# Attention mask of a tile written into two PSUM banks by VectorE and ScalarE in place of two matmuls

## The chip, the cores and the metric

The program runs on one core of a Trainium2 chip. The metric is the device time of one execution in microseconds (us). The engines that matter here are TensorE (PE in the profile, its weight loads PEld), VectorE (DVE), ScalarE (ACT), GpSimd (POOL) and the DMA queue that SyncE issues to (SPq). They run side by side, each through its own list of instructions in program order, and wait for each other by semaphores.

## What is computed

The reference is a chain of four residual blocks on x of 4 x 512 tokens x 128 channels. Two of the four are the same 6-layer stack of windowed attention and a gated MLP, and they take most of the time; only their attention matters for this change:

```
x = x + gla(layernorm(x)); x = x + stack(layernorm(x))
x = x + mamba(layernorm(x)); x = x + stack(layernorm(x))

# one attention layer of the stack: 16 heads of 64, windows of w = 32 tokens,
# each window's queries look at its own and the previous window's keys
mask = (it < jb) | (it > jb + w) | (jb == -1)
sim = jnp.einsum('bhwie,bhwje->bhwij', bq, bk2) * QK_SCALE
sim = jnp.where(mask, -jnp.finfo(sim.dtype).max, sim)
attn = jax.nn.softmax(sim, -1)
out = jnp.einsum('bhwij,bhwje->bhwie', attn, bv2)
```

The mask depends on the position inside the window alone, and on whether a window is the first of its sequence (it has no previous window). In the kernel a masked place gets -1e30 added.

## The kernel before

**The stack as units.** A stack handles 6 layers x 4 sequences = 24 iterations (`it`), each of 4 tiles of 128 tokens. One tile of one iteration is a unit `u`, so a stack has 96 units and the program 192. `pe_body`, `act_body`, `dve_body` and `pool_body` write out, for each engine, the work of one iteration. In the body of unit u stand pieces of several units, software-pipelined: the projections of q, k, v (`pe_proj`, chunks c = 0 to 5 of 512 columns, lines 273 to 275) of units u+2 and u+3, the transposes of q and k (`pe_qk_t`, line 286) and the scores (`pe_scores`, line 320) of unit u+1, and the transposed probabilities (`pe_probs_t`, line 301), the product with v (`pe_pv`, line 335) and the output projection (`pe_wo`, line 372) of units u and u-1. The MLP of the iteration before is spread over the same bodies (lines 378 to 403). The order is fixed by these functions; nothing is scheduled at run time.

**The banks.** PSUM has eight banks of 128 x 512 f32. `proj_ps` (banks 0, 1) takes the projection chunks in turn, `tr_ps` (2, 3) the transposes, `s_ps[0]` and `s_ps[1]` (4, 5) the scores of the even and of the odd heads of a unit, `o_ps` (6, 7) the rest.

**The scores of a unit.** `pe_scores(.., half 0)` waits until q and k of the unit stand transposed in SBUF (`qkT_ev`), and until the two score banks are free: `s_ps[0]` once VectorE has subtracted the row maximum (`sub_done`, line 775), `s_ps[1]` once ScalarE has taken the exponentials of the odd heads (`exp1_done`, line 571). Line 313 then starts each bank with a matmul of 512 columns: a one-hot matrix (it picks the row of the mask for each query) times the mask's rows, in bf16, one on the upper and one on the lower 64 rows of the array. 64 small matmuls of line 320 add the scores of four heads of each parity onto it, and 64 more (half 1) those of the others. VectorE then reduces both banks to the row maximum (line 770), ScalarE takes the exponentials (571, 578), VectorE sums and inverts (782, 786), GpSimd normalizes (934).

**v and the DMA queue.** `act_v` (line 535) copies the two v chunks of unit u+2 out of `proj_ps`; after the second, SyncE issues 16 DMAs (line 1035) that lay v out by window, and the first v copy of the next unit waits for them to land (`vp0` to `vp3`).

**The order around the change.** On ScalarE, in the body of u: copies of q transposed (554, `q_t`), the square of chunk 2 (527), the copies of k transposed (554, `k_t`), the square of chunk 3. On VectorE: rotation of chunk 1 (736, 738), the residual add (796, 797), rotation of chunks 2 and 3, the reciprocal norm (759 to 764), then the row maximum (770).

Of the kernel before, what the change touches and what calls it, by code (L numbers as in the profile page):

```python
# [20 lines left out]
BF16 = mybir.dt.bfloat16  # L21
I32 = mybir.dt.int32
ALU = mybir.AluOpType
ACT = mybir.ActivationFunctionType
# [54 lines left out]
def build(nc, a):  # L79

    ctx = ExitStack()
    with ctx:  # L82
# [13 lines left out]
        onehot = sb("onehot", [P, 2, P], BF16)  # L96
        maskrow = sb("maskrow", [P, CH], BF16)
        eps_t = sb("eps_t", [P, 1])
        rsq_3kk = sb("rsq_3kk", [P, 2 * HEADS])
        CONSTS = ((ident, "ident"), (center, "center"), (mean, "mean"), (onehot, "onehot"), (maskrow, "maskrow"))  # L100
# [103 lines left out]
        def mamba_buffers():  # L204
# [44 lines left out]
            "qkT_ev", "s_mm", "max_done", "sub_done", "den_sum", "exp1_done", "exp0_done", "den_done", "pT_mm", "pT_ev",  # L249
# [55 lines left out]

        def pe_scores(it, u, half):

            t = u % TILES
            if half == 0:
                nc.tensor.wait_ge(S["qkT_ev"], cnt(it, 4, u, 4))  # L310
                for g in range(2):
                    wait(nc.tensor, S["exp1_done" if g else "sub_done"], cnt(it, 1, u))
                    nc.tensor.matmul(s_ps[g], onehot[64 * g:64 * g + 64, 1 if t == 0 else 0, :],
                                     maskrow[64 * g:64 * g + 64, :], start=True, stop=False,
                                     skip_group_check=True)
# [264 lines left out]

        def act_center(e, src=o_ps[0]):
# [53 lines left out]
        def act_body(layer, j, mlp, ahead, more, norm=False):  # L635

            it = layer * B + j
            for u in range(TILES):
# [5 lines left out]
                if proj:  # L644
                    act_square(it, u + 2, 2)
                if nxt:
                    act_qk_t(it, u + 1, (2, 3))
# [130 lines left out]

        def dve_den(it, u):
# [54 lines left out]
        def dve_body(layer, j, mlp, ahead, norm=False):  # L834

            it = layer * B + j
            for u in range(TILES):
# [12 lines left out]
                elif prev:  # L850
                    dve_wo(it, u - 1)
                if proj:
                    dve_rotate(layer, j, u + 2, (2, 3))
# [953 lines left out]
def constants():  # L1807
# [22 lines left out]
    maskrow = np.zeros((64, HC, 2 * WIN), np.float32)  # L1830
    maskrow[:WIN] = np.concatenate([prev, own], 1)[:, None, :]
    maskrow[WIN, :, :WIN] = MASKED
    onehot = np.zeros((64, 2, P), np.float32)
    onehot[:WIN] = np.tile(np.eye(WIN), (1, WPT))[:, None, :]
    onehot[WIN, 1, :WIN] = 1.0
# [4 lines left out]
    for i in range(1, P // BC):  # L1840
        for n in range(BC):
            bc[i * BC + n, n, :] = 1.0
    return {"gla_pick": pick, "mb_bc_pick": bc.astype(bf), "rot": np.ascontiguousarray(rot), "maskrow": np.tile(maskrow.reshape(64, CH), (2, 1)).astype(bf),
            "onehot": np.tile(onehot, (2, 1, 1)).astype(bf), "ident": np.eye(P, dtype=np.float32),
# [62 lines left out]
```

## Time and profile before

| what | value |
|---|---|
| median of 3 runs | 3710.29 us (3702.14 to 3711.01) |
| the profiled execution, its own time | 3706.15 us |
| its span in the trace | 3704.4 us |
| mean granted TensorE clock, share of full | 0.978 |
| busy share of the span | PE 93%, PEld 67%, DVE 79%, ACT 74%, POOL 74% |

A busy share is an average over stages. The two stacks lie at about 140 to 1730 us and 2070 to 3680 us of the span; the other two blocks lie before and between them. A PE row's length is that of one instruction through the array, and instructions overlap in it, so what an instruction costs PE is read from the start of one row to the start of the next.

### The profile page before, as it was taken

What the parts mean: (1) busy time and instruction counts of PE and PEld (TensorE: products, weight loads), DVE (VectorE), ACT (ScalarE), POOL (GpSimd) and SP (SyncE); (2) the same over time, 40 slices, a digit from 0 to 9 for tenths busy, and PEclk for the clock granted to TensorE, in tenths of its full rate; (3) what the DMA queues carried; (4) which work ended last, traced back from release to release, by engine and by line L of the source; (5) the groups of instructions that cost most, each with busy time, mean ns of one, the idle gap of its engine ahead of it and who ended that gap; (6) DMA issues with size and microseconds to landing.
All of it is one profiled execution on the core that took longest, in us unless ns stands there. A gap on an engine that the chain in (4) does not pass through costs nothing. (4 is left out here: it accounts for less than half of the span.)

```text
span 3704.4 us, 152641 instructions
## 1 busy us (share of the span) xinstructions
PE 3447.7 (93%) x62652; PEld 2472.5 (67%) x62652; DVE 2934.0 (79%) x4676; ACT 2727.1 (74%) x7154; POOL 2739.4 (74%) x3122
## 2 busy tenths in 40 slices
PE   8799999999999999998887799999999999999996
PEld 3477777777777777775332577777777777777774
DVE  7688888888888888784999788888888878778773
ACT  2477878788787877776665578787787887777774
POOL 3587878787787878773666688787787878778772
PEclk9899999999999999999999899999999999999998
DMA  1232333333332333322000233332332333323321
GB/s 42 57 76 68 83 78 77 77 81 74 82 81 68 88 76 76 79 73 67 0 1 0 51 75 77 75 82 72 82 78 68 86 74 77 81 69 76 80 73 36
DMA packets 182839, 251.51 MB, mean 68 GB/s; under 512 B 53380, under 2 KB 74504, under 8 KB 182024
## 3 DMA queue, kind: packets, MB, share of 16 engines
q1 hardware_dynamic: 182152, 241.78, 26.2%
q8 instruction: 500, 8.19, 1.0%
q14 instruction: 187, 1.53, 0.1%
HBM read 39.20 MB, written 1.05 MB: 11 GB/s over the span
## 5 line engine op out<-in xcount | busy, mean ns | idle before, releaser
L959 POOL TENSOR_TENSOR qk_rows<-rot_products 128x512 f32<-128x512 f32 x768 | 983.0, 1281 | 223.2 <-DVE rot_products L736 222.6
L736 DVE TENSOR_TENSOR rot_products<-psum,rot_scaled 128x1024 f32<-128x1024 f32 x768 | 936.3, 1219 | 148.5 <-ACT squares L527 125.8
L969 POOL TENSOR_TENSOR qk_rows<-qk_rows,rnorm 128x512 f32<-128x512 f32 x768 | 803.7, 1078 | 15.0
L273 PE MATMUL psum<-wqkv_hi,xs_hi 128*128 128x512 f32 x1152 | 560.4, 486 | 89.3 <-DVE rot_products L736 37.3
L527 ACT ACTIVATE squares<-psum 128x512 f32<-128x512 f32 x768 | 488.4, 636 | 42.0 <-PE psum L275 36.6
L738 DVE TENSOR_REDUCE sumsq<-squares 128x8 f32<-128x512 f32 x768 | 518.2, 675 | 0.0
L535 ACT ACTIVATE v_rows<-psum 128x512 f32<-128x512 f32 x384 | 228.0, 595 | 367.8 <-DMA v_pairs<-v_rows 188.8
L934 POOL TENSOR_TENSOR probs<-probs,rden 128x512 f32<-128x512 f32 x384 | 393.3, 1045 | 92.4 <-DVE rden L786 91.5
L571 ACT ACTIVATE probs<-psum,minus_row_max 128x64 f32<-128x64 f32 x1536 | 457.1, 335 | 5.0 <-DVE minus_row_max L770 4.9
L275 PE MATMUL psum<-wqkv_hi,xs_lo 128*128 128x512 f32 x1152 | 459.6, 399 | 0.2 <-issue 0.2
L274 PE MATMUL psum<-wqkv_lo,xs_hi 128*128 128x512 f32 x1152 | 459.6, 399 | 0.0
L335 PEld LDWEIGHTS psum<-probs_t,v_pairs 64*64 64x64 f32 x24576 | 389.8, 136 | 103.0 <-issue 102.4
L335 PE MATMUL psum<-probs_t,v_pairs 64*64 64x32 f32 x24576 | 416.8, 221 | 27.7 <-issue 25.7
L372 PEld LDWEIGHTS psum<-o_t,wo 128*128 128x128 f32 x3072 | 362.9, 192 | 83.4 <-ACT o_t L543 60.3
L372 PE MATMUL psum<-o_t,wo 128*128 128x128 f32 x3072 | 388.2, 280 | 22.7 <-ACT o_t L543 16.4
L286 PE MATMUL psum<-ident,qk_rows 128*128 128x128 f32 x3072 | 402.9, 274 | 0.7 <-ACT q_t L554 0.5
L286 PEld LDWEIGHTS psum<-ident,qk_rows 128*128 128x128 f32 x3072 | 357.3, 142 | 29.9 <-issue 3.6
L320 PEld LDWEIGHTS psum<-k_t,q_t 64*32 64x32 f32 x24576 | 269.9, 105 | 151.4 <-issue 150.8
L571 ACT ACTIVATION_READ_ACCUMULATOR probs<-psum,minus_row_max 128x1 f32 x1536 | 353.8, 230 | 0.0
L273 PEld LDWEIGHTS psum<-wqkv_hi,xs_hi 128*128 128x128 f32 x1152 | 218.6, 190 | 187.6 <-issue 108.5
L320 PE MATMUL psum<-k_t,q_t 64*32 64x64 f32 x24576 | 332.4, 224 | 0.0
L770 DVE TENSOR_REDUCE minus_row_max<-psum 128x16 f32<-128x1024 f32 x192 | 234.3, 1220 | 115.9 <-PE psum L320 115.8
(188 smaller groups left out, 5995.3 us busy)
## 6 DMA issues: line engine op xcount, KB each, us to landing
v_pairs<-v_rows SPq DMA_DIRECT2D x3072, 64.0 KB, 2.0
wqkv_staged<-in_Wqkv SPq DMA_DIRECT2D x52, 384.0 KB, 3.6
wo<-in_Wo SPq DMA_DIRECT2D x12, 512.0 KB, 4.6
w<-in_W SPq DMA_DIRECT2D x12, 341.0 KB, 3.5
qk_scale<-in_qk_scale SPq DMA_DIRECT2D x12, 128.0 KB, 3.4
w<-in_W SPq DMA_DIRECT2D x12, 128.0 KB
mb_bc_pick<-in_mb_bc_pick SPq DMA_DIRECT2D x1, 1024.0 KB
out_x<-qk_rows SPq DMA_DIRECT2D x1, 1024.0 KB, 5.1
```

The lines of the kernel that those rows point to most:

```text
L273: nc.tensor.matmul(proj_ps[c % 2], xh, wh, start=True, stop=False)
L274: nc.tensor.matmul(proj_ps[c % 2], xh, wl, start=False, stop=False)
L286: last = nc.tensor.transpose(tr_ps[g % 2][:, i * P:(i + 1) * P], m["qk"][:, u % 2, (4 * g + i) * P:(4 * g + i + 1) * P], ident[:, :])
L320: last = nc.tensor.matmul(s_ps[par][WIN * w:WIN * w + WIN, 64 * hp:64 * hp + 64], m["qt"][rows, hp, WIN * w:WIN * w + WIN], m["kt"][rows, ...
L335: last = nc.tensor.matmul(o_ps[par][64 * j:64 * j + 64, P * (hp // 2) + WIN * w:P * (hp // 2) + WIN * w + WIN], m["vp"][rows, u % TILES, w ...
L372: last = nc.tensor.matmul(out[:, 0:P], m["wo"][:, hp, :], m["ot"][:, hp, :], start=(hp == 0), stop=(hp == HP - 1))
L527: nc.scalar.activation(m["sq"][:, c % 2, :], proj_ps[c % 2], ACT.Square).then_inc(S["sq_done"], 1)
L571: last = nc.scalar.activation(m["p"][:, hp, 1, :], s_ps[1][:, 2 * WIN * hp:2 * WIN * (hp + 1)], ACT.Exp, bias=m["mx"][:, 1, hp:hp + 1], ac ...
L736: V.tensor_tensor(m["mm"][:, c % 2, :, :].rearrange("p a (h e) -> p a h e", e=DH), ps, cos_sin, ALU.mult)\
L738: V.tensor_reduce(m["ss"][:, HC * c:HC * c + HC], m["sq"][:, c % 2, :].rearrange("p (h e) -> p h e", e=DH), AX.X, ALU.add)\
L959: G.tensor_tensor(qk[:, c * CH:(c + 1) * CH].rearrange(half, a=2, e=DH // 2), cos, sin[:, :, ::-1, :], ALU.add)\
L969: G.tensor_tensor(part, part, m["rn"][:, u % 2, HC * c:HC * c + HC].unsqueeze(2) .to_broadcast([P, HC, DH]), ALU.mult).then_inc(S["rot_don ...
```

## The change

The mask is now a constant of 128 partitions x 2 forms x 64 columns in f32 (`masks`; form 1 is for the first tile of a sequence), in place of the one-hot matrix and the mask's rows. For all units but the first of each stack, the two matmuls of line 313 are gone. In their place VectorE copies the mask, repeated for 8 heads, into `s_ps[0]` (`dve_mask`) and ScalarE copies it into `s_ps[1]` (`act_mask`), both in the body of the unit before, and the first score matmul waits for both copies (`mask_even`, `mask_odd`). The first unit of each stack starts both banks by an f32 matmul with the identity. The other score matmuls are unchanged and add onto what stands in the bank.

```diff
-        onehot = sb("onehot", [P, 2, P], BF16)
-        maskrow = sb("maskrow", [P, CH], BF16)
+        masks = sb("masks", [P, 2, 2 * WIN])
...
+        def fills(it, u):
+            return cnt(it, 1, u) - (it + u // TILES) // PHASE
+        def mask_of(u):
+            return masks[:, 1 if u % TILES == 0 else 0, :].unsqueeze(1).to_broadcast([P, HP, 2 * WIN])
...
                 nc.tensor.wait_ge(S["qkT_ev"], cnt(it, 4, u, 4))
-                for g in range(2):
+                if it % PHASE or u:
+                    nc.tensor.wait_ge(S["mask_even"], fills(it, u))
+                    nc.tensor.wait_ge(S["mask_odd"], fills(it, u))
+                for g in range(0 if it % PHASE or u else 2):
                     wait(nc.tensor, S["exp1_done" if g else "sub_done"], cnt(it, 1, u))
-                    nc.tensor.matmul(s_ps[g], onehot[64 * g:64 * g + 64, 1 if t == 0 else 0, :],
-                                     maskrow[64 * g:64 * g + 64, :], start=True, stop=False,
+                    nc.tensor.matmul(s_ps[g], ident[:, :], mask_of(u), start=True, stop=False,
                                      skip_group_check=True)
...
+        def act_mask(it, u):
+            nc.scalar.wait_ge(S["exp1_done"], cnt(it, 1, u))
+            nc.scalar.activation(s_ps[1].rearrange("p (h k) -> p h k", k=2 * WIN), mask_of(u), ACT.Copy)\
+                .then_inc(S["mask_odd"], 1)
...
                 if proj:
                     act_square(it, u + 2, 2)
+                if nxt:
+                    act_mask(it, u + 1)
                 if nxt:
                     act_qk_t(it, u + 1, (2, 3))
...
+        def dve_mask(it, u):
+            V.wait_ge(S["sub_done"], cnt(it, 1, u))
+            V.tensor_copy(s_ps[0].rearrange("p (h k) -> p h k", k=2 * WIN), mask_of(u)).then_inc(S["mask_even"], 1)
...
                 elif prev:
                     dve_wo(it, u - 1)
+                if nxt:
+                    dve_mask(it, u + 1)
                 if proj:
                     dve_rotate(layer, j, u + 2, (2, 3))
```

How the instructions stand on TensorE in the body of the first unit of an iteration, before (301 transposes the probabilities, 313 writes the mask, 320 are score matmuls):

```order
1063 L378 MATMUL psum<-x_ffn,center 128x512 [waits d1_ev]
1064 L301 MATMUL psum<-ident,probs 128x128 [waits qkT_ev,pn_done]
1065 L301 MATMUL psum<-ident,probs 128x128 x3
1066 L301 MATMUL psum<-ident,probs 128x128 [waits qkT_ev,pn_done]
1067 L301 MATMUL psum<-ident,probs 128x128 x3
1068 L313 MATMUL psum<-maskrow,onehot 128x512 [waits sub_done,qkT_ev]
1069 L313 MATMUL psum<-maskrow,onehot 128x512 [waits exp1_done]
1070 L320 MATMUL psum<-k_t,q_t 32x64 x32
```

The same place after the change, where the same source lines have other numbers (387 is 378, 300 is 301, 329 is 320):

```order
1039 L387 MATMUL psum<-x_ffn,center 128x512 [waits d1_ev]
1040 L300 MATMUL psum<-ident,probs 128x128 [waits qkT_ev,pn_done]
1041 L300 MATMUL psum<-ident,probs 128x128 x3
1042 L300 MATMUL psum<-ident,probs 128x128 [waits qkT_ev,pn_done]
1043 L300 MATMUL psum<-ident,probs 128x128 x3
1044 L329 MATMUL psum<-k_t,q_t 32x64 [waits mask_odd,mask_even,qkT_ev]
1045 L329 MATMUL psum<-k_t,q_t 32x64 x31
```

The two 512-column matmuls are gone from TensorE's list, and the wait for both banks now stands at the first score matmul. ScalarE before, from the copies of q transposed to the copies of the transposed probabilities:

```order
467 L554 ACTIVATE q_t<-psum 128x512 [waits qkT_mm,s_mm]
468 L554 ACTIVATE q_t<-psum 128x512 [waits qkT_mm]
469 L527 ACTIVATE squares<-psum 128x512 [waits red_done,qkv_mm]
470 L554 ACTIVATE k_t<-psum 128x4x128 [waits qkT_mm,s_mm]
471 L554 ACTIVATE k_t<-psum 128x4x128 [waits qkT_mm]
472 L527 ACTIVATE squares<-psum 128x512 [waits red_done,qkv_mm]
```

And ScalarE after, at the corresponding place of an iteration (563 is 554, 536 is 527):

```order
553 L563 ACTIVATE q_t<-psum 128x512 [waits qkT_mm,s_mm]
554 L563 ACTIVATE q_t<-psum 128x512 [waits qkT_mm]
555 L536 ACTIVATE squares<-psum 128x512 [waits red_done,qkv_mm]
556 L592 ACTIVATE psum<-masks 128x512 [waits exp1_done]
557 L563 ACTIVATE k_t<-psum 128x4x128 [waits qkT_mm,s_mm]
558 L563 ACTIVATE k_t<-psum 128x4x128 [waits qkT_mm]
```

One activation has come in ahead of the copies of k. VectorE after, from the rotation of chunk 1 on (752 and 754 are 736 and 738, 816 and 817 are 796 and 797, 775 is 759):

```order
621 L752 TENSOR_TENSOR rot_products<-psum,rot_scaled 128x1024 [waits add_done,sq_done]
622 L754 TENSOR_REDUCE sumsq<-squares 128x8
623 L816 TENSOR_TENSOR x_ffn<-psum,x_ffn 64x128 [waits d1_mm]
624 L817 TENSOR_TENSOR x_ffn<-psum,x_ffn 64x128
625 L797 COPY psum<-masks 128x512 [waits sub_done]
626 L752 TENSOR_TENSOR rot_products<-psum,rot_scaled 128x1024 [waits add_done,sq_done]
627 L754 TENSOR_REDUCE sumsq<-squares 128x8
```

The copy stands between the residual add and the rotation of chunk 2; without row 625 this is the order before. GpSimd's and SyncE's lists inside the stacks are the same before and after.

## Rows read from the trace of the kernel before

**Rows 1.** The page's first part: busy us, share of the span, instructions.

```profile
PE 3447.7 (93%) x62652; PEld 2472.5 (67%) x62652; DVE 2934.0 (79%) x4676; ACT 2727.1 (74%) x7154; POOL 2739.4 (74%) x3122
```

**Rows 2.** Busy time by stretch: window, us, busy by engine, PEclk, DMA share, GB/s.

```profile
400.00:1700.00 1300.00, 1260.54 (x25625) 953.81 (x25618) 1055.12 (x1735) 1029.78 (x2790) 1041.33 (x1207) 1.00 0.32 78
```

**Rows 3.** Timeline of PE: start, us, engine, line, op, tiles, count, idle before.

```profile
1076.71 1.03 PE L301 MATMUL psum<-ident,probs 128*128 128x128 f32 x8
1077.68 0.39 PE L313 MATMUL psum<-maskrow,onehot 64*128 64x512 bf16 x2
1078.00 0.86 PE L320 MATMUL psum<-k_t,q_t 64*32 64x64 f32 x64
...
1090.01 1.04 PE L286 MATMUL psum<-ident,qk_rows 128*128 128x128 f32 x8
1090.80 0.48 PE L273 MATMUL psum<-wqkv_hi,xs_hi 128*128 128x512 f32 x1
...
1095.72 0.39 PE L274 MATMUL psum<-wqkv_lo,xs_hi 128*128 128x512 f32 x1
1095.95 0.40 PE L275 MATMUL psum<-wqkv_hi,xs_lo 128*128 128x512 f32 x1
1096.28 0.86 PE L320 MATMUL psum<-k_t,q_t 64*32 64x64 f32 x64
```

**Rows 4.** Timeline of PE between chunk 5 and chunk 0, first body.

```profile
1081.90 0.39 PE L275 MATMUL psum<-wqkv_hi,xs_lo 128*128 128x512 f32 x1
1082.25 0.47 PE L273 MATMUL psum<-wqkv_hi,xs_hi 128*128 128x512 f32 x1
```

**Rows 5.** Timeline of ACT around the same place.

```profile
1067.12 0.60 ACT L535 ACTIVATE v_rows<-psum 128x512 f32<-128x512 f32 x1 [1.09 <-PE psum L275]
...
1073.72 0.69 ACT L527 ACTIVATE squares<-psum 128x512 f32<-128x512 f32 x1
1074.97 1.09 ACT L554 ACTIVATE k_t<-psum 128x512 f32<-128x512 f32 x2 [0.56 <-PE psum L286]
...
1080.61 0.60 ACT L535 ACTIVATE v_rows<-psum 128x512 f32<-128x512 f32 x1 [1.63 <-DMA v_pairs<-v_rows]
1081.11 0.68 ACT L605 ACTIVATE gelu<-psum,eps_t 128x512 f32<-128x512 f32 x1
```

**Rows 6.** Timeline of DVE: rotation of chunk 2, row maximum.

```profile
1075.13 1.22 DVE L736 TENSOR_TENSOR rot_products<-psum,rot_scaled 128x1024 f32<-128x1024 f32 x1
...
1081.46 1.23 DVE L770 TENSOR_REDUCE minus_row_max<-psum 128x16 f32<-128x1024 f32 x1 [0.86 <-PE psum L320]
```

**Rows 7.** Waits, 400 to 1700 us: total us, times, longest.

```profile
ACT v_rows L535 <- DMA v_pairs<-v_rows: 73.3, 38, 3.5
...
ACT k_t L554 <- PE psum L286: 48.4, 80, 1.7
...
DVE minus_row_max L770 <- PE psum L320: 45.3, 56, 0.9
...
PEld psum L372 <- ACT o_t L543: 26.0, 53, 1.8
...
PE psum L372 <- ACT o_t L543: 5.2, 10, 1.6
```

**Rows 8.** Groups of instructions: count, busy us, mean ns, idle before.

```profile
L1502 ACT ACTIVATE psum<-mb_dt_relu 128x512 f32<-128x512 f32 x8 | 4.8, 602 | 4.7 <-DVE mb_poly L1597 4.7
...
L1782 DVE COPY x_main<-psum 128x512 f32<-128x512 f32 x4 | 2.8, 692 | 9.4 <-PE psum L1736 9.3
...
L881 DVE TENSOR_SCALAR wqkv_hi<-wqkv_staged 128x768 fp32r<-128x768 f32 x4 | 2.2, 558 | 6.3 <-DMA wqkv_staged<-in_Wqkv 6.2
```

**Rows 9.** Timeline of PE: an f32 matmul of 512 columns; the first unit's mask.

```profile
1091.59 1.02 PE L394 MATMUL psum<-xn_mlp,w 128*128 128x512 f32 x2
1092.45 1.02 PE L395 MATMUL psum<-xn_mlp,w 128*128 128x512 f32 x2
...
154.32 0.39 PE L313 MATMUL psum<-maskrow,onehot 64*128 64x512 bf16 x2 [0.69 <-ACT k_t L554]
```

More of the change, by code:

```diff
@@ L95, in build @@
         mean = sb("mean", [P, P])
-        onehot = sb("onehot", [P, 2, P], BF16)
-        maskrow = sb("maskrow", [P, CH], BF16)
+        masks = sb("masks", [P, 2, 2 * WIN])
         eps_t = sb("eps_t", [P, 1])
         rsq_3kk = sb("rsq_3kk", [P, 2 * HEADS])
-        CONSTS = ((ident, "ident"), (center, "center"), (mean, "mean"), (onehot, "onehot"), (maskrow, "maskrow"))
+        CONSTS = ((ident, "ident"), (center, "center"), (mean, "mean"), (masks, "masks"))
         ln_xc = sb("ln_xc", [P, T])
@@ L248, in build @@
             "seed", "newton", "add_done", "rot_done", "v_ev", "vp0", "vp1", "vp2", "vp3", "pn_done", "oT_ev", "qkT_mm",
-            "qkT_ev", "s_mm", "max_done", "sub_done", "den_sum", "exp1_done", "exp0_done", "den_done", "pT_mm", "pT_ev",
+            "qkT_ev", "s_mm", "max_done", "sub_done", "mask_even", "mask_odd", "den_sum", "exp1_done", "exp0_done", "den_done", "pT_mm", "pT_ev",
             "o_mm", "wo_in", "w1_in", "w2_in", "vec_in", "qks_in", "rots_done", "d1_mm", "d1_ev",
@@ L1829, in constants @@
     own = np.where(tau[:, None] < tau[None, :], MASKED, 0.0)
[L1830 to L1835, printed above, removed]
+    masks = np.zeros((WPT, WIN, 2, 2 * WIN), np.float32)
+    masks[:] = np.concatenate([prev, own], 1)[None, :, None, :]
+    masks[0, :, 1, :WIN] = MASKED
     bf = mybir.dt.np(BF16)
@@ L1842, in constants @@
             bc[i * BC + n, n, :] = 1.0
-    return {"gla_pick": pick, "mb_bc_pick": bc.astype(bf), "rot": np.ascontiguousarray(rot), "maskrow": np.tile(maskrow.reshape(64, CH), (2, 1)).astype(bf),
-            "onehot": np.tile(onehot, (2, 1, 1)).astype(bf), "ident": np.eye(P, dtype=np.float32),
+    return {"gla_pick": pick, "mb_bc_pick": bc.astype(bf), "rot": np.ascontiguousarray(rot), "masks": masks.reshape(P, 2, 2 * WIN), "ident": np.eye(P, dtype=np.float32),
             "center": (np.eye(P) - 1.0 / P).astype(np.float32), "mean": np.full((P, P), 1.0 / P, np.float32)}
```

## The prediction

> **What bounds the kernel now.** I read the busy shares first. TensorE is busy for 93% of the span, no other engine for more than 79% [rows 1]; in a long stretch of the first stack it is 1260.5 of 1300 us, with VectorE at 1055, ScalarE at 1030 and GpSimd at 1041, and the clock fully granted [rows 2]. The reader is to see that TensorE leads, and that each of the others has some 240 to 270 us of 1300 free: 80 units fall into that stretch (the 80 waits of `k_t`, one to a unit [rows 7]), so a unit lasts 1300 / 80 = 16.25 us, and VectorE is idle for (1300 − 1055) / 80 = 3.1 us of it, ScalarE for 3.4.
>
> Second, the timeline, to see whether TensorE's busy time is work. Neighbours of 512 columns start 0.23 us apart (1095.72 to 1095.95) though each row is 0.39 to 0.40 us long [rows 3]: the rows overlap, and a gap of less than 0.2 us doesn't show as idle. The Trainium skill, "Trainium Kernel Development and Optimization", section Performance Expectations, warns of just this: matmul busy time is a bad measure of how near a kernel is to its limit, the busy share of the weight loads a better one. By that rule TensorE would stand at 67% here and a matmul taken out might be worth nothing, which is the third rival below; by the starts of the rows it works through most of a unit without a hole, which is what I go by.
>
> Third, the table of waits, for who paces TensorE where it does wait. Two places count. The output projection waits for ScalarE's copy of the attention output 53 + 10 = 63 times in 80 units, 31.2 us in all, 0.39 us a unit [rows 7]. And ScalarE's first v copy waits for the DMAs of the unit before 38 times, 73.3 us [rows 7]. The second is a loop that TensorE is not in: the second v copy ends at 1067.72, the DMAs are issued and land, and the next first v copy starts at 1080.61, 12.9 us later [rows 5]; in the first body of an iteration ScalarE's logarithm follows it, ends at 1081.11 + 0.68 = 1081.79, and TensorE's chunk 0, which waits for it, starts at 1082.25, 0.35 us after its neighbour instead of 0.23 [rows 4, 5].
>
> **What is removed.** Line 313 occurs in 192 units; it stays (in another form) in 2, so 190 pairs go. A pair's cost is from its start to the next one's: 1077.68 to 1078.00, 0.32 us [rows 3]. Beside it, the eight transposes ahead of it take 0.97 us (1076.71 to 1077.68), where eight equal transposes ahead of a projection take 0.79 (1090.01 to 1090.80): 0.18 us goes into changing over to the half-array matmul. A change into the small score matmuls is needed afterwards too; at another place it costs 0.33 − 0.23 = 0.10 us (1095.95 to 1096.28 against 1095.72 to 1095.95) [rows 3]. So a unit's gain lies between 0.32 us (the 0.18 stays) and 0.40 (0.97 + 0.32 becomes 0.79 + 0.10). I take 0.36; over 190 units 68 us, with 61 and 76 as ends.
>
> **What of it reaches the end.** An iteration has four bodies, and in each the removed pair lies between two points; it counts only if TensorE's own work leads from the one to the other. Over the six-layer stacks the bodies u = 0, 1, 2 occur 48 times each, u = 3 46 times (the last has no next unit).
> - u = 0: the pair lies ahead of chunk 0 at 1082.25, which is set by the DMA loop and the logarithm [rows 4, 5]. TensorE would arrive earlier and wait for as much longer: nothing.
> - u = 1: the DMA loop runs on through this body (second v copy of the first body, 16 DMAs, first v copy of the next), and the output projection waits for ScalarE's chain behind it in part of the iterations. I count half.
> - u = 2 and u = 3: here v copies wait for TensorE (as the one at 1067.12, idle 1.09 us for chunk 5 [rows 5]), so ScalarE's chain and the DMAs start earlier when TensorE is earlier: all.
>
> That is 0 + 24 + 48 + 46 = 118 units x 0.36 = 42.5 us. A cross-check from the waits: the DMA ends the v copy's wait in 38 of 80 units; if just the other 42 gained, it would be 190 x 42/80 = 100 units, 36 us.
>
> **What is added on VectorE.** One copy of 128 x 512 f32 a unit. A copy of this size out of PSUM takes 0.69 us; the one-source operation between two SBUF tiles takes 0.56 us for 768 columns, 0.37 for 512 [rows 8]. I take 0.69, as the destination is PSUM, and keep 0.37. It goes in ahead of the rotation of chunk 2, where VectorE has no idle time (1075.13), so all behind it is 0.69 us late: both rotations, the norm, and with them GpSimd. It is given back at the row maximum, which now waits 0.86 us for TensorE (1081.46) [rows 6], 45.3 us in 56 of the 80 units, 0.81 each [rows 7]. TensorE comes 0.36 earlier there, so 0.81 − 0.36 = 0.45 covers the most part and 0.24 stays; the maximum ends at 1082.69, and ScalarE's exponentials come behind a v copy, a logarithm and more, so the 0.24 is hidden too. I take 0. If the cover were gone in all units: 190 x 0.24 = 46 us.
>
> The Trainium skill, "SBUF — State Buffer", section Who interferes with whom, says that a VectorE copy in a two-port mode shuts GpSimd out for its length. As it also asks for source and destination in SBUF, it would not apply to this copy; if it did, GpSimd would lose up to 0.37 us a unit, of which it has 3.2 idle by the windows. No row here shows such a copy into PSUM.
>
> **What is added on ScalarE.** One activation from SBUF to PSUM of 128 x 512: 0.60 us, by the same kind of operation [rows 8]. It stands ahead of the copies of `k_t`, which now wait for TensorE's transposes 80 times for 48.4 us, 0.605 each [rows 7], 0.56 in the example [rows 5]. Nothing in between on TensorE is removed, so this cover doesn't shrink. I take 0; queued behind it are the two `k_t` copies, chunk 3's square and the copies of the probabilities, and TensorE's transposes of the probabilities wait for `k_t`. Where the idle time is under 0.60, they are late by the difference.
>
> **The waits.** TensorE's first score matmul waits for both copies. They end at about 1075.8 and 1075.0, and the scores start at 1078.00 [rows 3, 5, 6]: over 2 us to spare. No price.
>
> **The first units.** Two f32 matmuls with the identity, 0.86 us each (1091.59 to 1092.45), against 0.32: +1.4 us, twice, where the scores are waited for (0.69 idle ahead of them) [rows 9]: +2.8, between 0 and 2.8; I take +2.
>
> **The sum.** 3706.15 (the profiled execution; span 3704.4, 1.75 us around it) − 42.5 + 2 = 3666 us. The execution lies 0.1% under the median of 3710.29, which I leave out.
>
> **Rivals.**
> - *All of it counts.* If the DMA loop moves with TensorE, since its start in the last body does, and the logarithm is no barrier, all 190 units gain: 3706 − 61 to 76 + 2 = 3632 to 3647. For it: TensorE is 97% busy in the stretch. Against it: the 38 DMA waits, and chunk 0 tied to the logarithm.
> - *ScalarE's copy comes on the path: slower.* The place is ahead of `k_t`. ScalarE's chain sets the output projection in 63 of 80 units and TensorE's transposes and copies follow on it; if the idle time before `k_t` doesn't take the 0.60 us, each unit is late by 0.60 and gains 0.36: 190 x 0.24 = +46, 3752 us. It decides from the point where the idle time falls below 0.60 − 0.36 = 0.24 us; the mean is 0.605, so I hold it unlikely. A shortfall of 0.1 us would cost 19 us.
> - *No gain, the others pace it.* If in all bodies the output projection is tied to ScalarE and through it to the DMAs, TensorE's saved time turns into waiting: 3706, at best −0.36 x 46 + 2, 3691. For it: 63 of 80. Against it: v copies waiting for TensorE.
>
> **Chances.** The forecast as reckoned (3655 to 3685) 0.5, all of it 0.13, no gain 0.22, slower 0.10, the small remainder 0.05. The likeliest is 3666; its own range is 3655 to 3685. With the neighbours taken in, 3640 to 3704 should hold it 8 times in 10. What a measurement can tell is 0.3%, 11 us: faster than 3699 us 0.70, within 3699 to 3721 0.17, slower 0.13.
>
> **What would show it.** In the profile after: no row of line 313's kind in the bodies, and 0.89 to 0.97 us from the first transpose of the probabilities to the first score matmul. A copy on VectorE of 0.69 us, on ScalarE of 0.60. The idle time before `k_t` and before the row maximum nearly gone. The v copy's wait for the DMAs longer and more frequent, and TensorE's wait for the logarithm too. The prediction would be wrong if the iteration (four bodies) is not shorter by about 0.9 us, if `k_t` makes TensorE's transposes wait, or if the wait at the output projection grows by as much as was saved.

## The result, and the profile after

The changed kernel takes 3683.92 us (median of 4 runs, 3681.94 to 3685.72) against 3709.55 of the kernel before (4 runs, 3702.14 to 3711.01): a ratio of 0.9925, 95% interval 0.9905 to 0.9945. That is 25.6 us, 0.69%, with 20 to 35 us as the interval; the forecast was 40. The profiled execution took 3684.87 us, its span 3683.1 at a mean clock of 0.975. The line numbers of after differ from those of before: 300 is 301, 329 is 320, 272 to 274 are 273 to 275, 381 is 372, 544 is 535, 552 is 543, 563 is 554, 786 is 770, 619 is 605; 592 and 797 are the new copies on ScalarE and VectorE.

The page's first part, and the same stretch as in [rows 2]:

```profile
PE 3405.5 (92%) x62276; PEld 2454.7 (67%) x62276; DVE 3054.4 (83%) x4866; ACT 2822.9 (77%) x7344; POOL 2743.4 (74%) x3122
```

```profile
400.00:1700.00 1300.00, 1249.36 (x25583) 951.50 (x25577) 1113.20 (x1820) 1074.83 (x2885) 1043.46 (x1208) 0.99 0.32 79
```

TensorE has 42 us less busy time in the span than in [rows 1], VectorE 120 more, ScalarE 96 more; TensorE has 376 instructions fewer, VectorE and ScalarE 190 more each, as the change says. The granted clock of the stretch is 0.99 where it was 1.00; this small difference matters and comes back below.

**The removed pair.** The timeline of TensorE in the first body of an iteration (u = 0; start, length, engine, line, op, tiles, count, idle before), which answers to [rows 3] and [rows 4]:

```profile
1073.88 1.03 PE L300 MATMUL psum<-ident,probs 128*128 128x128 f32 x8
1074.84 0.86 PE L329 MATMUL psum<-k_t,q_t 64*32 64x64 f32 x64
...
1078.74 0.40 PE L274 MATMUL psum<-wqkv_hi,xs_lo 128*128 128x512 f32 x1
1080.79 0.47 PE L272 MATMUL psum<-wqkv_hi,xs_hi 128*128 128x512 f32 x1 [1.65 <-ACT gelu L619]
...
1085.82 0.40 PE L274 MATMUL psum<-wqkv_hi,xs_lo 128*128 128x512 f32 x1
1086.70 2.02 PE L381 MATMUL psum<-o_t,wo 128*128 128x128 f32 x16 [0.49 <-ACT o_t L552]
```

The transposes take 0.96 us to the next start, as before the pair (0.97), so the 0.18 us of changing over stayed, and the pair's 0.32 us went: 190 x 0.32 = 61 us of TensorE's own time. Two places show it given back: chunk 0 waits 1.65 us for the logarithm (before it started 0.35 us after its neighbour), and the output projection 0.49 for ScalarE (before 0.18).

**The copies and their cover.** ScalarE at the same place, beside [rows 5], and VectorE, beside [rows 6]:

```profile
1070.96 0.69 ACT L536 ACTIVATE squares<-psum 128x512 f32<-128x512 f32 x1
1071.43 0.71 ACT L592 ACTIVATE psum<-masks 128x512 f32<-128x512 f32 x1
1072.14 1.09 ACT L563 ACTIVATE k_t<-psum 128x512 f32<-128x512 f32 x2
...
1079.15 0.60 ACT L544 ACTIVATE v_rows<-psum 128x512 f32<-128x512 f32 x1 [3.01 <-PE psum L274]
1079.64 0.68 ACT L619 ACTIVATE gelu<-psum,eps_t 128x512 f32<-128x512 f32 x1
```

```profile
1072.37 0.69 DVE L797 COPY psum<-masks 128x512 f32<-128x512 f32 x1
1073.09 1.23 DVE L752 TENSOR_TENSOR rot_products<-psum,rot_scaled 128x1024 f32<-128x1024 f32 x1
...
1078.47 1.22 DVE L786 TENSOR_REDUCE minus_row_max<-psum 128x16 f32<-128x1024 f32 x1
```

Neither `k_t` nor the row maximum shows idle time ahead of it now, where they had 0.56 and 0.86 us. Over the whole run, by groups (count, busy us, mean ns, idle us before):

```profile
L786 DVE TENSOR_REDUCE minus_row_max<-psum 128x16 f32<-128x1024 f32 x192 | 233.7, 1217 | 14.7 <-PE psum L329 13.1 <-issue 0.2
L563 ACT ACTIVATE k_t<-psum 128x512 f32<-128x512 f32 x384 | 208.8, 595 | 30.6 <-PE psum L285 27.4 <-issue 0.3
```

Before, the same groups read 115.9 us and 126.4 us of idle time. The copies took up 101 and 96 us of it. For ScalarE that is 0.50 us a copy, less than its row of 0.71: the square's row begins at 1070.96 and lasts 0.69 us, the copy's begins at 1071.43, so the rows overlap, and a copy takes less of the engine's time than its length. The copies' own lengths, shortest, median and longest in ns:

```profile
L592 ACT ACTIVATE psum<-masks x190: 595/710/724, 165.6 to 3613.4; 128x512 f32<-128x512 f32 x190
L797 DVE COPY psum<-masks x190: 685/695/697, 167.1 to 3617.0; 128x512 f32<-128x512 f32 x190
```

**The waits,** 400 to 1700 us (total us, times, longest), beside [rows 7]:

```profile
ACT v_rows L544 <- DMA v_pairs<-v_rows: 85.4, 48, 3.2
...
ACT v_rows L544 <- PE psum L274: 50.7, 51, 3.0
...
PEld psum L381 <- ACT o_t L552: 29.0, 53, 1.2
...
PE psum L272 <- ACT gelu L619: 17.1, 16, 1.8
...
PE psum L381 <- ACT o_t L552: 6.9, 12, 0.9
PEld psum L403 <- DVE hidden L832: 5.8, 19, 0.3
```

The v copy waits for the DMAs 48 times instead of 38. The weight loads of the output projection wait for ScalarE 29.0 us instead of 26.0; the row of its matmuls (6.9, before 5.2) lies in the same units and is the same wait, so the two aren't added. TensorE's wait for the logarithm ahead of chunk 0 (`gelu` L619) is 17.1 us in 16 times, where it was 10.8 in 11. The last row is new: a chunk of the up-projection now waits for VectorE. The row of v copies that wait for TensorE needs care. The one at 1079.15 [3.01] stands in it, though its chunk had ended at about 1076.6 (the chunk of 1076.20). What it waited for was again the transfers: SyncE's own row reads

```profile
1064.96 11.03 SPq L1057 DMA_DIRECT2D v_pairs<-v_rows  x16
```

so the last of the 16 was issued at 1075.40 to 1075.99. Transfers take 2.0 us at the median to land; the trace has this one, the slowest of the 16, landed at 1079.05, and the v copy began 0.10 us later. Issuing alone, at 0.69 us apiece, makes 11 us of the loop from one unit's second v copy to the next unit's first.

**The bodies.** The interval from one output projection to the next, sorted by the body whose pair lies in it; means in us over both stacks but their first and last iterations:

| kernel | u=0 | u=1 | u=2 | u=3 | iteration | iterations with a lower clock | the others |
|---|---|---|---|---|---|---|---|
| before | 16.93 | 15.46 | 17.35 | 16.02 | 65.76 | 2 | 65.60 |
| e1, before with both copies | 16.62 | 15.59 | 17.32 | 16.03 | 65.56 | 4 | 65.32 |
| e10, two pairs | 16.92 | 15.62 | 17.49 | 16.23 | 66.26 | 4 | 66.09 |
| after | 16.60 | 15.49 | 17.18 | 15.73 | 65.00 | 4 | 64.74 |
| e2, no pair and no copies | 16.84 | 15.39 | 17.06 | 15.73 | 65.02 | 5 | 64.72 |
| e3, after without VectorE's copy | 17.01 | 15.33 | 17.10 | 15.75 | 65.19 | 8 | 64.69 |
| e4, after without ScalarE's copy | 16.89 | 15.37 | 17.11 | 15.71 | 65.08 | 7 | 64.65 |
| e7, after, VectorE's copy moved | 17.07 | 15.32 | 17.14 | 15.74 | 65.27 | 10 | 64.60 |
| e5, before, loop open | 16.04 | 15.37 | 17.48 | 16.03 | 64.92 | 2 | 64.75 |
| e6, after, loop open | 15.80 | 15.44 | 17.18 | 15.69 | 64.11 | 2 | 64.03 |
| e8, after, loop open, copy moved | 15.77 | 15.37 | 17.05 | 15.72 | 63.91 | 3 | 63.73 |
| e9, e2 with the loop open | 15.99 | 15.37 | 17.11 | 15.72 | 64.19 | 9 | 63.64 |

The experiments e1 to e12 follow below; "loop open" means that the first v copy no longer waits for all transfers. The last two columns count, of the 44 iterations, those in which TensorE's clock was lowered for a while, and give the mean of the rest. Only u = 3 moves by the full 0.3 us and without scatter. The means of u = 0 and u = 1 scatter by some 0.2 us and more from one execution to the next: the five closed-loop kernels without the pair (after, e2, e3, e4, e7) have 16.60 to 17.07 at u = 0, mean 16.88, and the two with one pair (before, e1) 16.93 and 16.62. By the means of those five against before the gain is 0.05, 0.08, 0.23 and 0.29 us for u = 0 to 3, 0.65 an iteration, 31 us over 48. Against e1, which has the pair too and takes the same time as before, u = 0 would read a loss of 0.26 and u = 1 a gain of 0.21, so these two bodies are not resolved one by one.

**The clock.** In its wait for the logarithm TensorE stands still, and in some iterations its granted clock falls right behind this wait, from 2.4 to 1.2 GHz. One such place in the changed kernel, and the same work at the full clock in another iteration:

```profile
1272.19 0.40 PE L274 MATMUL psum<-wqkv_hi,xs_lo 128*128 128x512 f32 x1
1274.39 0.66 PE L272 MATMUL psum<-wqkv_hi,xs_hi 128*128 128x512 f32 x1 [1.81 <-ACT gelu L619]
...
1275.84 3.64 PE L344 MATMUL psum<-probs_t,v_pairs 64*64 64x32 f32 x128
1279.40 0.79 PE L272 MATMUL psum<-wqkv_hi,xs_hi 128*128 128x512 f32 x1
```

```profile
1081.65 2.07 PE L344 MATMUL psum<-probs_t,v_pairs 64*64 64x32 f32 x128
1083.65 0.50 PE L272 MATMUL psum<-wqkv_hi,xs_hi 128*128 128x512 f32 x1
```

The 128 matmuls take 1279.40 − 1275.84 = 3.56 us there against 2.00. The trace's record of the clock shows 1.00 until 1274.5 and 0.50 for 6.8 us from there; the stretch of 1274 to 1281 us reads 0.54 on average.

In the eight profiles with the loop closed there are 43 such stretches, of 3.4 to 10.2 us, inside the iterations counted above, and 37 of them begin within 2.5 us of chunk 0's start, where chunk 0 started 1.8 to 2.6 us after the matmul ahead of it; in the iterations without such a stretch this distance is 0.9 to 1.3 us on average. An iteration with such a stretch lasts 2 to 4 us longer on average.

The kernel before has them in 2 of its 44 iterations, e1 in 4, the five without the pair in 4 to 10. Over all executions the mean granted clock is 0.976 for the kernel before (55 runs), 0.973 for the five kernels without the pair (31 runs), and 0.977 for e5, e6, e8 and e9 with the loop open (21 runs). So where TensorE's saved time turned into waiting, the wait was sometimes followed by slower work, and part of the gain was lost that way: by the profiles (6.8 such iterations on average against 3, 2.6 us each) about 11 us over the two stacks, an estimate. That the lower clock follows from the longer wait is read from these places; no run changed the clock alone, and long waits occur without it too.

### The profile page after: what moved, and what is told of

It reads as the page before. It is cut to its first block and busy times, and to the rows that moved or that the text cites. A ratio compares the mean times of both kernels' runs of the same rounds, so it can differ in the third digit from the quotient of the medians.

```text
span 3683.1 us, 152268 instructions
## 1 busy us (share of the span) xinstructions
PE 3405.5 (92%) x62276; PEld 2454.7 (67%) x62276; DVE 3054.4 (83%) x4866; ACT 2822.9 (77%) x7344; POOL 2743.4 (74%) x3122
## 5 line engine op out<-in xcount | busy, mean ns | idle before, releaser
L991 POOL TENSOR_TENSOR qk_rows<-qk_rows,rnorm 128x512 f32<-128x512 f32 x768 | 813.1, 1090 | 15.0
L344 PE MATMUL psum<-probs_t,v_pairs 64*64 64x32 f32 x24576 | 418.3, 221 | 30.6 <-issue 28.7
L570 ACT ACTIVATE probs_t<-psum 128x512 f32<-128x512 f32 x384 | 208.2, 599 | 125.3 <-PE psum L300 125.2
```

Of the source, the lines that this page charges most:

```text
L344: last = nc.tensor.matmul(o_ps[par][64 * j:64 * j + 64, P * (hp // 2) + WIN * w:P * (hp // 2) + WIN * w + WIN], m["vp"][rows, u % TILES, w ...
L991: G.tensor_tensor(part, part, m["rn"][:, u % 2, HC * c:HC * c + HC].unsqueeze(2) .to_broadcast([P, HC, DH]), ALU.mult).then_inc(S["rot_don ...
```

## The experiments

The theory behind the prediction, A: TensorE's saved time counts only where TensorE leads; in the other bodies the loop over the v copies and their DMAs sets the pace, with ScalarE in it, and the copies are hidden. The rivals: B, VectorE's copy costs what is missing; C, ScalarE's copy does. Ratios are to the kernel before, with 95% intervals.

### The two halves of the change apart

**e1.** The kernel before with both copies added and the matmuls kept, which overwrite what the copies wrote.

```diff
+                if nxt:
+                    act_mask(it, u + 1)      # ScalarE, ahead of k_t; waits and order as in the changed kernel
...
+                if nxt:
+                    dve_mask(it, u + 1)      # VectorE, ahead of the rotation of chunk 2
```

> The kernel before, with both matmuls of the mask kept and the two copies added at their places ahead of them (the values copied are overwritten by the matmuls; their source is 64 columns of another constant). It prices the copies alone. Theory A (the copies are free, TensorE's saved time is lost to the DMA loop and ScalarE's pace): within 5 us of the kernel before, 3705 to 3715. Theory B (VectorE's copy makes the MLP's hidden product, and TensorE behind it, late by about 0.3 us once an iteration): about 48 x 0.3 = 14 us slower, 3720 to 3727, with TensorE waiting for the hidden product ahead of the third up-projection. Theory C (ScalarE's copy is what costs, at the copies of k): slower by 15 us or more, with TensorE waiting for ScalarE ahead of the transposed probabilities.

Measured: 3708.75 us (12 runs), ratio 0.9994 (0.998 to 1.0008). Two copies a unit cost nothing that shows while TensorE has its pair; the interval leaves at most 3 us, and theory B's 14 and C's 15 are excluded for this kernel.

**e2.** The kernel before with the pair taken out and nothing in its place; it leaves out the mask.

```diff
-                    nc.tensor.matmul(s_ps[g], onehot[64 * g:64 * g + 64, 1 if t == 0 else 0, :],
-                                     maskrow[64 * g:64 * g + 64, :], start=True, stop=False,
...
-                            start=False, stop=True, skip_group_check=True)
+                            start=True, stop=True, skip_group_check=True)
```

> The kernel before without the two mask matmuls and without any copy; the score matmuls start their own places, so the mask is left out of the computation. It prices the removal alone. Theory A: the same as the changed kernel, 3684 us give or take 5. Theory B: about 14 us faster than the changed kernel, 3668 to 3674. Theory C: faster than the changed kernel by 15 us or more. If all of the removed time counted it would be 192 x 0.32 = 61 us, 3648; that is expected by none.

Measured: 3679.57 us (6 runs), ratio 0.9908 (0.9881 to 0.9934), 31 us (24 to 44) of the 61, as theory A said. So about half of the removed time doesn't count even where no copy was added. Its waits, 400 to 1660 us:

```profile
ACT v_rows L532 <- DMA v_pairs<-v_rows: 80.5, 44, 3.3
...
PE psum L273 <- ACT gelu L602: 17.1, 14, 1.9
```

The DMA row has grown as in the changed kernel, and TensorE waits 17.1 us for the logarithm, as much as there.

**e10.** The other way round: the pair issued twice, the second pair writing the same values over the first.

```diff
+                for g in range(2):
+                    nc.tensor.matmul(s_ps[g], onehot[64 * g:64 * g + 64, 1 if t == 0 else 0, :],
+                                     maskrow[64 * g:64 * g + 64, :], start=True, stop=False,
```

> The kernel before with the pair of mask matmuls issued twice in each of the 192 units, which adds 0.21 to 0.32 us of TensorE's time a unit, 41 to 61 us. Theory A (half of TensorE's time counts, since in the first bodies it waits for the loop): by the first order 20 to 35 us slower, 3730 to 3745, and more than half of it if the added time fills the slack of 0.84 us only in part. Rival (TensorE leads, and the removal alone fell short only by noise): the whole 41 to 61 us, 3750 to 3770.

Measured: 3728.63 us (9 runs), ratio 1.0052 (1.0032 to 1.0071). TensorE's timeline:

```profile
1015.65 0.39 PE L313 MATMUL psum<-maskrow,onehot 64*128 64x512 bf16 x2
1015.87 0.38 PE L317 MATMUL psum<-maskrow,onehot 64*128 64x512 bf16 x2
1016.18 0.86 PE L324 MATMUL psum<-k_t,q_t 64*32 64x64 f32 x64
```

Both pairs take 1016.18 − 1015.65 = 0.53 us, so the second adds 0.21, 192 x 0.21 = 40 us. It cost 19.9 us by the medians (12 to 26): about half, as with the removal. A microsecond of TensorE is worth about half a microsecond in this kernel, in both directions.

### Each copy left out

**e3** and **e4.** The changed kernel without VectorE's copy, and without ScalarE's; each leaves out the mask of half of the heads.

```diff
# e3
-                    dve_mask(it, u + 1)
# e4
-                    act_mask(it, u + 1)
```

> The changed kernel without VectorE's copy: the even heads get no mask, their score matmuls start their own places. ScalarE's copy stays. Theory A: 3684, as the changed kernel. Theory B: as with the matmuls alone removed, about 3670, and no wait for the hidden product. Theory C: 3684.

> The changed kernel without ScalarE's copy: the odd heads get no mask, their score matmuls start their own places. VectorE's copy stays. Theory A: 3684. Theory B: 3684, with TensorE's wait for the hidden product unchanged. Theory C: about 3670 or less.

Measured: 3690.26 us (6 runs), ratio 0.9938 (0.9916 to 0.9961), and 3690.55 (8 runs), ratio 0.9932 (0.9908 to 0.9956). Neither is faster than the changed kernel (0.9925), and the intervals leave no room for the 14 us of B or the 15 of C; both fall for the kernel as it is.

**e7.** The changed kernel with VectorE's copy one place earlier, ahead of the sums.

```diff
+                if nxt:
+                    dve_mask(it, u + 1)
                 dve_den(it, u)
```

> The changed kernel with VectorE's copy moved ahead of the sum of the exponentials, where VectorE waits about 1 us for ScalarE in three of four bodies. Theory A: TensorE's wait for the hidden product (5.8 us in 19 of 80 units) goes, but the other holders stay: within 6 us of the changed kernel, 3678 to 3690. Theory B (that wait is what the u = 2 gain was lost to): 48 x 0.3 = 14 us faster, 3667 to 3673.

Measured: 3685.30 us (7 runs), ratio 0.994 (0.9918 to 0.9962): no difference from the changed kernel by the total. The median interval of u = 2 shows what the total can't: it is 17.05 us in after and in e4, which have VectorE's copy ahead of the rotation, and 16.91 to 16.93 in e2, e3 and e7, which don't. The new wait of the up-projection (5.8 us, 19 times) is there in after and e4 and missing in the other three. The two kernels with the pair, before and e1, have 17.22 there. VectorE's copy makes its product for the MLP (`hidden`) late, and that costs 0.12 us in u = 2; without it, u = 2 gains 0.29 to 0.31, nearly the whole slot. That the total doesn't show it fits with the loop and the lower clock (10 iterations in e7's profile) taking it back, which isn't shown.

### The loop opened

**e5** and **e6.** Of a unit's 16 DMAs two read the half of the v buffer that the next first v copy overwrites. They are issued first, with a semaphore of their own, and the v copy waits for these two alone. e5 does it to the kernel before, e6 to the changed one.

```diff
+            for half, w, par in sorted((half, w, par) for half in range(2) for w in range(WPT) for par in range(2)):
...
+                SP.dma_start(...).then_inc(S["v_old"] if old else vp_sem[t], 16)
...
-                wait(nc.scalar, vp_sem[(u - 1) % TILES], it * PAIRS + PAIRS * ((u - 1) // TILES + 1))
+                wait(nc.scalar, S["v_old"], 32 * cnt(it, 1, u))
```

> The kernel before, with the DMA loop opened: the two of the 16 DMAs of a unit that read the older half of the v buffer are issued first and have a semaphore of their own, and the next unit's first v copy waits for these two alone (and for all 16 of the unit before that one). Theory A (the loop v copy, DMAs, v copy paces TensorE in the first bodies): the v copy's waits for DMAs nearly go, and so does TensorE's wait for the logarithm; 0.84 us of 65.5 an iteration is lost there and up to 0.7 at the two places behind it, so 20 to 60 us faster than the kernel before, 3650 to 3690. Rival R (ScalarE's own chain or GpSimd sets the pace, the DMAs are only the last to be waited for): within 8 us of the kernel before.

> The changed kernel with the same opened loop. Theory A: now all four removed matmul pairs of an iteration count, so it is faster than e5_before_loop_open by 50 to 61 us (190 x 0.32), where the changed kernel is 26 faster than the one before: 3595 to 3635. Rival R: the same 26 us as without the opening, about 3684 or 26 below e5. In between (35 to 45 below e5): the loop is one of two holders, the other being ScalarE's exponentials ahead of the output projection or VectorE's late hidden product.

Measured: 3669.47 us (6 runs), ratio 0.9891 (0.9871 to 0.9912), and 3637.53 (5 runs), ratio 0.9802 (0.9779 to 0.9824). The loop alone was worth 39 us (33 to 48); the rival that the transfers are only the last to be waited for allowed 8 and falls. With the loop open the change brings 32 us instead of 26. With some 11 us of uncertainty on the 32 this is not told apart from the 26, which was the rival's figure; it is short of the 50 to 61 that A by itself would give. The waits of e6, 400 to 1660 us:

```profile
ACT v_rows L545 <- PE psum L274: 86.1, 107, 1.1
...
PEld psum L382 <- ACT o_t L553: 22.8, 45, 0.8
...
PEld psum L300 <- POOL probs L957: 7.6, 16, 0.6
...
PEld psum L404 <- DVE hidden L833: 4.7, 18, 0.3
```

No v copy waits for DMAs, and the longest wait for TensorE has fallen from 3.0 to 1.1 us, which confirms that the long ones of the changed kernel were transfers. Two waits are left that come from VectorE: the transposes for GpSimd's normalizing, which waits for VectorE's sums, and the up-projection for `hidden`.

**e8.** e6 with VectorE's copy moved as in e7.

> The changed kernel with the opened loop and VectorE's copy moved. If the hidden product holds TensorE once the loop does not, it is faster than e6_after_loop_open by 8 to 14 us; if not, the same within 5 us. A candidate for the best version.

Measured: 3626.84 us (5 runs), ratio 0.9776 (0.9755 to 0.9797), 10.7 us under e6 by the medians. The intervals of the ratios overlap a little, but four of the five runs of e8 lie under the fastest of e6 (3629.37). Its waits:

```profile
ACT v_rows L545 <- PE psum L274: 82.0, 100, 1.2
...
PEld psum L382 <- ACT o_t L553: 23.1, 47, 0.5
...
PE psum L382 <- ACT o_t L553: 1.5, 6, 0.3
PEld psum L300 <- POOL probs L957: 1.4, 6, 0.2
```

The wait for `hidden` is gone and that for GpSimd down to 1.4 us.

**e9.** e2 with the loop open: no pair, no copies, no mask.

> The kernel before with the DMA loop opened and the two mask matmuls removed without any copy (the mask is left out of the computation). It asks how much of the 61 us counts once the loop is open, with no copy in the way. The kernel with the loop open and the matmuls kept took 3669, with the copies and VectorE's moved 3627. Theory A: 3669 - 61 = 3608, give or take 6; then the copies cost the other 18 us of e8_both. Rival (ScalarE's exponentials ahead of the output projection hold TensorE in part whatever the copies do): 3620 to 3630, as e8_both.

Measured: 3626.61 us (5 runs), ratio 0.9767 (0.9743 to 0.9792), the same as e8, as the rival expected. So the copies cost nothing that shows once VectorE's is moved, and about 10 us where it was put. But it missed the 3608 of theory A: 43 us of the 61 count with the loop open, not all. Part of the missing 18 goes with the clock: e9's runs were granted 0.9762 on average, those of e5 0.9785, and e9's profile has 9 iterations with a lower clock against 2. In the other iterations e9 is faster than e5 by 64.75 − 63.64 = 1.11 us, which is 53 us over 48.

**e11.** e8 with the odd heads' bank written by VectorE too.

```diff
+            V.wait_ge(S["exp1_done"], cnt(it, 1, u))
+            V.tensor_copy(s_ps[1].rearrange("p (h k) -> p h k", k=2 * WIN), mask_of(u)).then_inc(S["mask_odd"], 1)
...
-                    act_mask(it, u + 1)
```

> The version with the opened loop and VectorE's copy moved (3627 us), with the copy into the odd heads' bank taken from ScalarE and made by VectorE right behind the other, 0.69 us more on VectorE and 0.71 less on ScalarE. If ScalarE's chain ahead of the output projection held it: up to 10 us faster, 3617. If VectorE has no room (it sums the exponentials right behind): up to 190 x 0.4 = 76 us slower by GpSimd's late normalizing. I expect 3625 to 3650.

Measured: 3642.23 us (5 runs), ratio 0.982 (0.9795 to 0.9845), 15 us over e8 and inside the 3625 to 3650 expected. Splitting the copies between two engines is worth that much. That VectorE has cover for one copy and not for two is the likely reading; which of the instructions behind it pays isn't shown.

**e12.** In e5, e8 and e9 alike the output projection waits for ScalarE's copy of the attention output, 22 to 24 us in this stretch (its weight loads). e12 is e8 with this copy issued ahead of the even heads' exponential.

```diff
+                if not norm:
+                    act_out_t(it, u)
+                if nxt:
                     act_exp_even(it, u + 1)
...
+                if norm:
                     act_out_t(it, u)
```

> The kernel is e8 (opened loop, VectorE's mask copy moved), with ScalarE's copy of the attention output issued ahead of the even heads' exponential instead of behind it. In e8 the output projection waited for that copy 23.1 us in 47 waits (and 1.5 us in 6 more) between 400 and 1660 us. Theory: once the loop through the transfers is open, ScalarE's order ahead of the output projection is what still keeps part of the removed TensorE time from counting. Then those waits go, and the time falls by 15 to 40 us below e8: 3590 to 3612 us. Rival: the even heads' exponential is itself late by the copy's length (about 0.6 to 1.1 us), so the sums, GpSimd's normalizing and the first probs transposes come later and wait in its place; then 3622 to 3645 us, with new waits of the probs transposes for GpSimd.

Measured: 3617.42 us (6 runs, 3608.39 to 3627.84), ratio 0.9758 (0.9735 to 0.9781). That lies between the two expectations: 9.4 us under e8 by the medians, but the kernel before, timed beside each of them, was also faster beside e12 (3702.98 against 3708.85 beside e8), and by the ratios it is 7 us, with overlapping intervals, so this gain is not shown. Its waits tell more:

```profile
PEld psum L404 <- issue: 10.7, 30, 0.6
...
PEld psum L272 <- ACT squares L537: 6.1, 4, 1.8
...
PEld psum L413 <- DVE x_ffn L822: 5.5, 16, 0.5
PEld psum L388 <- DVE x_ffn L822: 5.1, 15, 0.4
PEld psum L300 <- POOL probs L961: 3.3, 10, 0.4
PEld psum L382 <- ACT o_t L553: 1.2, 3, 0.7
```

The 23.1 us of the weight loads at the output projection are down to 1.2. In e8 the rows of `x_ffn` don't occur, `squares` reads 1.9, L404 3.7 and `probs` 1.4; together these grew by some 24 us. With the exponentials later, VectorE's sums are late: GpSimd's normalizing waits 53.9 us for them, where it waited 23.2 in e8. Most of the wait did not vanish, it went to other places; the largest of them, the 10.7 us at L404, the trace puts down to no engine. e12 has the lowest time of all versions, 2.4% under the kernel before.

## Why the prediction was right in its direction and too high in its size

- **The slot, 0.36 us a unit: mis-sized.** It was the middle between 0.32 (the changeover stays) and 0.40 (it goes). The trace shows the lower end: 0.96 us of transposes and 0.32 saved. 118 x 0.04 = 4.7 us of the miss.
- **u = 0, nothing: right.** Five kernels without the pair have a mean of 16.88 us there against 16.93 and 16.62 (before, e1), and TensorE's wait for the logarithm grew from 10.8 us (11 times) to 17.1 (16 times).
- **The clock: not in the sum.** The prediction read it as fully granted and put nothing for it. The longer wait at u = 0 was followed more often by a stretch at the lower clock, which took back some 11 us by the estimate above.
- **u = 1, half: not resolved.** The five means give 0.08 us against before, a quarter of the slot, and 0.21 against e1. The term was 24 units; 12 to 31 fit.
- **u = 2, all: the step that failed.** It kept 0.17 us of 0.32 in the profile after and 0.23 over the five. The cause is that VectorE's copy makes `hidden` late (0.12 us, by the medians of e2, e3 and e7 against after and e4), which the prediction had costed at nothing by looking at the row maximum alone. The waits of the output projection for ScalarE grew too, from 26.0 to 29.0 us; in which bodies they cost something isn't shown.
- **u = 3, all: right,** 0.29 of 0.32.
- **The sum redone** with what was measured: (0.05 + 0.08 + 0.23 + 0.29) x 48 = 31 us, less 2.8 for the first units, is 28; 25.6 by the medians. Over iterations at the full clock alone the five are 64.68 on average against 65.60 (before) and 65.32 (e1), 31 to 44 us over 48, so what those iterations gained doesn't contradict the forecast's 40. The slot, u = 2 and the clock were all missed in the same direction, and the measured 3683.92 lies at the very end of the stated range of 3655 to 3685: the mechanism was right, but that the number came out inside is partly luck. The single pair of profiles shows less, 21.3 us of span; between the first and last output projection of each stack it is 27.0, the rest lies before and between the stacks.
- **ScalarE's copy, 0.60 us: 0.71 as a row, 0.50 of the engine's time,** still within the cover of `k_t`, whose idle time fell from 126.4 to 30.6 us. Cost nothing: right (e1, e4).
- **VectorE's copy, 0.69 us: 0.695.** Cost nothing: right for the total with the loop closed (e1, e3), wrong in u = 2, and about 10 us once the loop is open (e6 against e8, e9).
- **The wait for both copies:** no row of it among the waits. Right.
- **The output projection's wait, 63 times in 80 units: misread.** The 10 waits of its matmuls lie in the same units as 10 of the 53 of its weight loads, so it is 53 units and 26.0 us, 0.33 a unit. The sum doesn't use the figure; the two rivals that rest on ScalarE looked stronger by it than they were.
- **The first units, +1.4 us each:** right. Both kernels around the first unit's mask, the changed one first:

```profile
154.26 1.99 PE L323 MATMUL psum<-masks,ident 128*128 128x512 f32 x4 [0.69 <-ACT k_t L563]
156.18 1.58 PE L329 MATMUL psum<-k_t,q_t 64*32 64x64 f32 x128
157.68 0.50 PE L272 MATMUL psum<-wqkv_hi,xs_hi 128*128 128x512 f32 x1
```

```profile
154.64 1.75 PE L320 MATMUL psum<-k_t,q_t 64*32 64x64 f32 x128
156.32 0.50 PE L273 MATMUL psum<-wqkv_hi,xs_hi 128*128 128x512 f32 x1
```

From the mask's start to the next projection it is 157.68 − 154.26 = 3.42 us against 156.32 − 154.32 = 2.00 (its start in [rows 9]).

Of the rivals, "all of it counts" and "no gain" were both half true: the loop through the DMAs held back part (39 us come from opening it, and then 43 of the 61 count, e5 and e9), VectorE's copy another (e6, e8). "Slower by ScalarE's copy" fell with e1. The weight loads' 67% as the measure of TensorE, which the Trainium skill, "Trainium Kernel Development and Optimization", section Performance Expectations, recommends, was read in the prediction as a possible gain of nothing: the runs show about half of the removed time gained, so it was neither idle time nor fully on the path. What stays open is how the 18 us that don't count with the loop open divide between the clock and ScalarE: e12 moved ScalarE's wait rather than removing it, and no run held the clock fixed.

## What to carry to other kernels

When one engine is 93% busy and the others 75 to 80%, removing work from it isn't worth its length: go body by body, and count it only between two points where that engine leads. For a sharper number, first double the work and see what that costs, since here doubling and removing both gave about half. Look for loops that the busiest engine isn't in, such as a buffer that is refilled only after all transfers have landed: here 2 of 16 transfers mattered, and letting the others go was worth more than the change. Price an added instruction at every consumer behind it on its engine, not only at the next wait that could absorb it. And where saved time on TensorE turns into a longer wait, look at the granted clock behind this wait: compare iterations with and without a lowered clock before a missing gain is put down to another engine.

## What the runs showed of the hardware

- Two 512-column matmuls on the upper and the lower 64 rows of the array take 0.32 us together from the first one's start to the next matmul's; a second such pair behind the first adds 0.21 us (e10). Of the 0.32, some 0.10 is the change from them to the small score matmuls. The eight transposes ahead take 0.97 us before this pair (190 times) and 0.97 before the small matmuls directly (190 times in the changed kernel), against 0.79 before a projection: leaving the full array costs 0.18 us whichever of the two smaller shapes is next.
- TensorE's granted clock fell in some iterations from 2.4 to 1.2 GHz for 3.4 to 10.2 us, in 37 of 43 places beside a wait in which no matmul started for 1.8 to 2.6 us; 128 small matmuls took 3.56 us in one such place and 2.00 at the full clock.
- ScalarE's copy of a repeated 64-column source from SBUF into PSUM takes 0.71 us at the median, where the activation from SBUF to PSUM of the same size in [rows 8] takes 0.60; the shortest of the 190 is 0.595.
- VectorE's copy into PSUM doesn't hold GpSimd up: 190 copies of 0.695 us are 132 us, and GpSimd's busy time went from 2739.4 to 2743.4 us. The group of `qk_rows` took 1281 ns on average before, and in the changed kernel:

```profile
L981 POOL TENSOR_TENSOR qk_rows<-rot_products 128x512 f32<-128x512 f32 x768 | 984.1, 1283 | 221.5 <-DVE rot_products L752 215.4
```

- Values that ScalarE and VectorE wrote into a bank, here 0 and -1e30, are added onto by score matmuls without a start, in all units but the first of each stack. That matmuls of the first unit had opened the banks is how the kernel is written; no run left it out.
- The releaser of a wait can be named wrongly by a coincidence: the v copy at 1079.15 began just as the next chunk's last matmul (1078.74) ended, and its 3.01 us were put down to that one, while the last transfer had landed at 1079.05.
